# Multiplying the first tile's keys while the key and value weights are still being turned

## The chip, the cores and the metric

One NeuronCore of a Trainium2 chip runs the whole kernel as one launch. The metric is the device time of that launch in microseconds (us). All times of the profile are microseconds from the start of its span unless marked ns.

## The reference

One layer of a graph transformer over 3125 nodes of width 1024 and 50,000 edges. The part that matters here is the linear attention's key and value stage, which comes first in the kernel:

```
xn = layernorm(x)
K = elu(xn @ Wk.T + bk) + 1           # 16 heads of 64
V = xn @ Wv.T + bv
KV = einsum('phd,phe->hde', K, V);  Ksum = K.sum(over nodes)
# later: Q, the mix with Wo; a graph attention over the edges; a feed forward with
# a piecewise linear gelu; each added to x
```

The graph attention uses a dense 3125 x 3125 matrix of edge counts in DRAM. It is built beside the key and value stage: 39 MB are filled with zeros and then every edge is added by indirect DMAs.

## The kernel before

The kernel is a row of blocks. Within a block each engine runs its own program and engines meet only at semaphores; at the end of a block all engines meet, and none starts the next block before the last has drained. Three blocks matter.

**The preparation block** (line 494). The weights Wk and Wv come as 16 blocks of 128 rows x 1024 (8 of each), into a ring of five places in SBUF (`raw`). TensorE turns a block with 8 transposes into a place in PSUM (`SplitWeights.turn`, L428), ScalarE copies a rounded high part (`take_high`, L292), VectorE then takes the rest, the low part (`take_low`, L296). There are three PSUM places (`places=3`), so block r is turned only when the low part of block r-3 has been taken. SyncE loads blocks 5 to 15, each when the place in the ring is free (`load`). In the same block the first tile of 125 rows of x is normalised, turned (`turn_rows`, L283) and split (`take`, L476 and L292; the low part is L296 on `xT_space`), and the edges' keys are made and turned (L574). SyncE also broadcasts the biases bk and bv and loads the rows of tile 1 (L508 to L509).

**The key and value block** (line 589) runs over 25 tiles. For each, TensorE makes `k_ps` (`project`, 48 matmuls of 512 columns: 8 blocks x 3 products of high and low parts x 2 halves), half of `v_ps` (24), turns the next tile's rows (8 transposes), makes the other half of `v_ps` (24) and `kv` (8 pairs). VectorE normalises the next tile, adds biases, sums, and prepares one unit of edges a tile (`Edges.prepare`, its last instruction is L354). GpSimd first issues 50 zero fills of 764 KB each (L617, four in flight), then the diagonal (L621 and L624), and then 47 batches of edges, two batches to a unit, with four indirect DMAs each (`scatter_unit`, `scatter_batch`, L360 to L375). Batch n+1 waits until batch n has landed.

**The query block** (line 749) follows, with the rest of the edge batches.

PSUM in the preparation block: three places of two banks for blocks and `tr`, two banks. In the key and value block: `tr`, `k_ps`, `v_ps` and `kv`, two banks each.

Of the kernel before, what the change touches and what calls it, by code (L numbers as in the profile page):

```python
# [19 lines left out]
D = 1024  # L20
# [4 lines left out]
T = 125  # L25
NT = N // T
KB = D // 128
FB = F // 128
CH = 128
# [424 lines left out]
def keys_and_values(nc, st, a):  # L454
# [12 lines left out]
    stats, moments, root = sb("stats", [T, 2, 6]), sb("moments", [T, 2]), sb("root", [T, 5])  # L467
    x_loaded, xn_ready, stats_seen, first_link = [sem(f"x_loaded{i}") for i in range(2)], sem("xn_ready"), sem("stats_seen"), sem("first_link")
    turned, xT_copied, xT_high, xT_low, rows_loaded = sem("turned"), sem("xT_copied"), sem("xT_high"), sem("xT_low"), sem("rows_loaded")
    tr = ps("tr", [128, KB, 128])  # L470
    EARLY = 4

    def take(act, g, slot):

# [5 lines left out]
    with ExitStack() as pst:  # L480
        psb, pps, psem = allocators(nc, pst, "KP")
        spare_i = psb("spare_i", [CH, BATCH], I32)
        src_c, dst_c = (edges.row[0:CR, i * CB * CH:(i + 1) * CB * CH].bitcast(I32).rearrange("p (b c) -> p b c", b=CB) for i in range(2))
        key_c = edges.row[0:CR, 0:CB * CH].rearrange("p (b c) -> p b c", b=CB)
        zeros_set, ident_zeroed, ident_ready = psem("zeros_set"), psem("ident_zeroed"), psem("ident_ready")
        pads_set = psem("pads_set")
        masks_set, masks_ready, sums_zeroed = psem("masks_set"), psem("masks_ready"), psem("sums_zeroed")
        edges_loaded, keys_made, keys_turned, keys_copied = (
            psem("edges_loaded"), psem("keys_made"), psem("keys_turned"), psem("keys_copied"))
        keys_stored = a["keys_stored"]  # L490
        weights = SplitWeights(nc, pst, "KW", ((a["wk"], wk), (a["wv"], wv)), ident, [raw[:, i, :] for i in range(5)], places=3)
        blocks = range(2 * KB)

        with nc.Block() as block:  # L494
            @block.sync
            def _(sp):
                load_rows(sp, rows[:, 0, :], a["x"][0:T, :], x_loaded[0])
                for tile, e in ((src_c, a["src"]), (dst_c, a["dst"])):
                    most, whole = (CB - 1) * CR * CH, CHUNKS * CH
                    sp.dma_start(tile[:, 0:CB - 1, :], e[0:most].rearrange("(b c p) -> c b p", c=CR, p=CH)).then_inc(edges_loaded, 16)  # L500
                    sp.dma_start(tile[0:PADS, CB - 1, :], e[most:whole].rearrange("(c p) -> c p", p=CH)).then_inc(edges_loaded, 16)
                sp.wait_ge(pads_set, 2)
                for tile, e in ((src_c, a["src"]), (dst_c, a["dst"])):
                    sp.dma_start(tile[PADS:PADS + 1, CB - 1, 0:REST], e[whole:E].rearrange("(c p) -> c p", c=1)).then_inc(edges_loaded, 16)
                weights.load(sp, range(weights.ring, len(blocks)))
                for tile, row, n in ((bk_row, a["bk"], 12), (bv_row, a["bv"], 13)):
                    sp.wait_ge(weights.turned, n)
                    sp.dma_start(tile[:, :], row.partition_broadcast(T)).then_inc(rows_loaded, 16)  # L508
                load_rows(sp, rows[:, 1, :], rows_of(a["x"], 1), x_loaded[1])  # L509
                sp.wait_ge(keys_stored, 16)  # L510

            @block.gpsimd
            def _(pool):
                nc.gpsimd.memset(ident[:, :], 0.0).then_inc(ident_zeroed, 1)
                nc.gpsimd.memset(edges.mask[:, 0:BATCH - 1, :], AGAIN).then_inc(masks_set, 1)
                nc.gpsimd.memset(edges.mask[:, BATCH - 1:2 * BATCH - 1, :], 1.0).then_inc(masks_set, 1)
                nc.gpsimd.iota(spare_i[:, :], pattern=[[CH, BATCH]], base=N * N, channel_multiplier=1).then_inc(masks_set, 1)
                pool.wait_ge(ident_zeroed, 1)
                nc.gpsimd.affine_select(out=ident[:, :], in_=ident[:, :], compare_op=ALU.not_equal, fill=1.0,
                                        base=0, pattern=[[-1, 128]], channel_multiplier=1).then_inc(ident_ready, 1)  # L520
                pool.wait_ge(masks_set, 3)
                own = edges.mask[:, BATCH - 1, :]
                nc.gpsimd.affine_select(out=own, in_=own, compare_op=ALU.is_ge, fill=AGAIN,
                                        base=0, pattern=[[1, CH]], channel_multiplier=-1).then_inc(masks_ready, 1)
                nc.gpsimd.tensor_copy(edges.spare[:, :], spare_i[:, :]).then_inc(masks_ready, 1)
                nc.gpsimd.memset(kv_sum[:, :, :], 0.0).then_inc(sums_zeroed, 1)
                nc.gpsimd.memset(k_sum[:, :], 0.0).then_inc(sums_zeroed, 1)
                pool.wait_ge(keys_made, 1)
                pool.dma_start(a["keys_dram"].rearrange("(b c p) -> c b p", b=CB, p=CH), key_c[:, :, :]).then_inc(keys_stored, 16)
                pool.wait_ge(masks_ready, 2)  # L530
                pool.wait_ge(sums_zeroed, 2)

            @block.scalar
            def _(act):
                weights.load(act, range(weights.ring))
                weights.take_high(act, range(EARLY))
                take(act, 0, 0)
                weights.take_high(act, range(EARLY, KB))
                act.wait_ge(keys_turned, 1)
                nc.scalar.activation(edges.keys[:, :].rearrange("p (b c) -> p b c", b=CB), tr[0:CH, 0:CB, 0:CR], ACT.Copy).then_inc(keys_copied, 1)  # L540
                weights.take_high(act, range(KB, len(blocks)))
                act.wait_ge(zeros_set, 1)

            @block.vector
            def _(dve):
                nc.vector.memset(src_c[PADS:CR, CB - 1, :], N).then_inc(pads_set, 1)
                nc.vector.memset(dst_c[PADS:CR, CB - 1, :], 0).then_inc(pads_set, 1)
                nc.vector.memset(zeros[:, :], 0.0).then_inc(zeros_set, 1)
                chain = Chain(dve, first_link)
                dve.wait_ge(x_loaded[0], 32)  # L550
                normalise(nc, chain, rows[:, 0, :], rows[:, 0, :], stats, moments, root, stats_seen).then_inc(xn_ready, 1)
                weights.take_low(dve, range(EARLY // 2))
                dve.wait_ge(edges_loaded, 96)
                nc.vector.scalar_tensor_tensor(out=key_c[:, :, :], in0=src_c[:, :, :], scalar=float(N), in1=dst_c[:, :, :],
                                               op0=ALU.mult, op1=ALU.add).then_inc(keys_made, 1)
                weights.take_low(dve, range(EARLY // 2, EARLY))
                dve.wait_ge(xT_high, 1)
                low(nc, xT[:, 0, 1, :, :], xT_whole[:, :, :], xT[:, 0, 0, :, :]).then_inc(xT_low, 1)
                weights.take_low(dve, range(EARLY, len(blocks)))
                dve.wait_ge(keys_copied, 1)  # L560
                dve.wait_ge(xn_ready, 1)
                dve.wait_ge(weights.low_ready, len(blocks))

            @block.tensor
            def _(pe):
                pe.wait_ge(ident_ready, 1)
                weights.turn(pe, range(EARLY))
                pe.wait_ge(xn_ready, 1)
                turn_rows(nc, tr, rows[:, 0, :], ident, turned)
                weights.turn(pe, range(EARLY, KB))  # L570
                pe.wait_ge(xT_copied, 1)
                pe.wait_ge(keys_made, 1)
                for b in range(CB):
                    last = nc.tensor.transpose(tr[0:CH, b, 0:CR], key_c[:, b, :], ident[0:CR, 0:CR])  # L574
                last.then_inc(keys_turned, 1)
                weights.turn(pe, range(KB, len(blocks)))


    ones = sb("ones", [T, NT, 1])
    k_ps, v_ps, kv = ps("k_ps", [128, D]), ps("v_ps", [128, D]), ps("kv", [128, KB, 128])  # L580

    xT_stored = sem("xT_stored")
    k_done, v_done, kv_done = sem("k_done"), sem("v_done"), sem("kv_done")
    kb_ready, k_low, k_exp, k_ready, v_ready = sem("kb_ready"), sem("k_low"), sem("k_exp"), sem("k_ready"), sem("v_ready")
    ones_set, diagonal_set = sem("ones_set"), sem("diagonal_set")
    zero_filled = [sem(f"zero_filled{i}") for i in range(FILLS_AHEAD)]
# [2 lines left out]
    with nc.Block() as block:  # L589
# [99 lines left out]
        def _(pe):  # L689
            def body(g, n):  # L690
                xT_now = xT[:, n % 2, :, :, :]
                pe.wait_ge(xT_low, g + 1)
                project(nc, k_ps, xT_now, wk, k_done)
                project(nc, v_ps, xT_now, wv, v_done, (0,))
                if fixed(g, 0, NT - 2):
                    pe.wait_ge(xn_ready, g + 2)
# [6 lines left out]
                    cols = slice(pair * 128, (pair + 1) * 128)  # L703
                    m = nc.tensor.matmul(kv[:, pair, :], v[:, cols], k[:, cols], start=True, stop=True)
                m.then_inc(kv_done, 1)
            over_tiles(pe, body)


def linear_attention(nc, st, a):
# [1230 lines left out]
```

## Time and profile before

| | us |
|---|---|
| median of three runs | 3107.56 (3103.63 to 3111.19) |
| the profiled execution, its own time | 3111.14 |
| its span | 3109.0 |
| TensorE, busy share of the span | 98% |
| VectorE | 84% |
| ScalarE | 37% |
| GpSimd | 26% |

Busy shares are averages over the whole span. The change is in the first 50 us, and GpSimd is busy only in the first 1300 us, so the reading has to be by stage. An engine's queue (PEq, POOLq, SPq) has entries of its own: DRAIN is an engine that has reached the end of its block and waits for its own work to finish, EVENT_SEMAPHORE its release into the next block.

### The profile page before, as it was taken

To read this page: it belongs to the slowest core of one execution; us is meant where nothing else is said; L and a number is where in the kernel's file an instruction comes from. 1 tells how busy PE (TensorE), PEld (TensorE's weight loads), DVE (VectorE), ACT (ScalarE), POOL (GpSimd) and SP (SyncE) were. 2 spreads that over 40 slices of the span, in tenths; PEclk is the share of its full clock that TensorE was granted. 3 is DMA by queue.
4 is the path that set the end of the run, shared out by engine and by line. 5 is a ranking of instruction groups with operands and counts; after the bars stand their busy time and mean duration, and the time that the engine had idled before them with its cause. 6 is when DMAs were issued, how large, how long until landed. Compare 5 with 4: busy or idle time off the path is not lost. (4 is left out here: it accounts for less than half of the span.)

```text
span 3109.0 us, 41236 instructions
## 1 busy us (share of the span) xinstructions
PE 3037.5 (98%) x14012; PEld 2500.3 (80%) x14012; DVE 2604.5 (84%) x4513; ACT 1164.5 (37%) x1499; POOL 803.3 (26%) x716
## 2 busy tenths in 40 slices
PE   8999999989999999899999999999999999999998
PEld 6888888867888888677778888888888888878887
DVE  6777777767777777698989999999999988788886
ACT  3111111122111111233346566556656644565554
POOL 1256666754655666200000000000000000000000
PEclk9999999999999999999999999999999999999999
DMA  9943333353444444555655356447446634233331
GB/s 341 374 99 65 60 60 60 73 134 71 84 93 93 80 93 93 159 167 170 184 165 161 112 154 167 128 127 202 123 121 168 168 93 118 75 88 106 104 106 53
DMA packets 184432, 395.83 MB, mean 127 GB/s; under 512 B 78181, under 2 KB 79061, under 8 KB 184310
## 3 DMA queue, kind: packets, MB, share of 16 engines
q1 hardware_dynamic: 106230, 308.58, 33.6%
q0 software_dynamic: 71440, 65.24, 11.4%
q10 hardware_dynamic: 6640, 20.45, 2.0%
q8 instruction: 68, 1.11, 0.2%
q14 instruction: 54, 0.44, 0.0%
HBM read 303.36 MB, written 90.81 MB: 127 GB/s over the span
## 5 line engine op out<-in xcount | busy, mean ns | idle before, releaser
L1580 PE MATMUL G_acc<-values,whole_plain 125*125 125x257 f32 x5000 | 1095.9, 381 | 15.8 <-DVE whole_plain L1524 8.6
L1580 PEld LDWEIGHTS G_acc<-values,whole_plain 125*125 125x125 f32 x5000 | 935.4, 188 | 166.0 <-DVE whole_plain L1524 11.8
L375 POOL DMA_INDIRECT counts<-E_twins_now,E_cells_now x392 | 672.9, 1717 | 308.6 <-DMA counts<-E_twins_now,E_cells_now 171.3
L1424 ACT ACTIVATE whole_plain<-whole_plain,G_asrc_slope 125x750 f32<-125x750 f32 (+1 forms) x400 | 377.6, 945 | 388.3 <-DVE whole_plain L1511 387.3
L1511 DVE SCALAR_TENSOR_TENSOR whole_plain<-whole_plain,G_asrc_most 125x750 f32<-125x750 f32 (+1 forms) x400 | 409.5, 1024 | 32.8 <-PE G_acc L1580 31.7
L1396 POOL DMA_DIRECT2D gat<-xT_plain x100 | 53.7, 537 | 1027.4 <-ACT xT_plain L1440 1027.4
L268 PE MATMUL V_v_ps<-whole,xT_space 128*125 128x512 f32 x1200 | 285.1, 399 | 8.0 <-DVE xT_space L296 4.0
L268 PE MATMUL Q_mm<-Q_mixer,xT_space 128*125 128x512 f32 x1200 | 284.8, 396 | 5.5 <-DVE xT_space L296 5.5
L268 PE MATMUL K_k_ps<-whole,xT_space 128*125 128x512 f32 x1200 | 287.1, 398 | 3.2 <-PEq L494 3.2
L1052 DVE SCALAR_TENSOR_TENSOR N_least<-xT_plain,asrc_all,N_least 125x750 f32<-125x750 bf16 (+1 forms) x292 | 289.7, 992 | 0.0
L268 PE MATMUL K_v_ps<-K_wv,xT_space 128*125 128x512 f32 x1200 | 287.9, 395 | 0.0
L268 PE MATMUL Q_q_ps<-whole,xT_space 128*125 128x512 f32 x1200 | 287.4, 398 | 0.0
L1524 DVE SCALAR_TENSOR_TENSOR whole_plain<-whole_plain 125x750 f32<-125x750 f32 (+1 forms) x288 | 277.3, 963 | 6.8 <-ACT whole_plain L1424 4.5
L268 PEld LDWEIGHTS V_v_ps<-whole,xT_space 128*125 128x125 f32 x1200 | 221.5, 187 | 70.3 <-DVE xT_space L296 11.9
L268 PEld LDWEIGHTS Q_mm<-Q_mixer,xT_space 128*125 128x125 f32 x1200 | 223.6, 186 | 62.5 <-DVE xT_space L296 6.0
L343 DVE SCALAR_TENSOR_TENSOR E_scratch<-E_row,E_col,E_mask 128x512 bf16<-128x512 f32 x392 | 267.8, 747 | 1.7
L268 PEld LDWEIGHTS K_k_ps<-whole,xT_space 128*125 128x125 f32 x1200 | 221.7, 186 | 58.6 <-issue 3.4
L268 PEld LDWEIGHTS Q_q_ps<-whole,xT_space 128*125 128x125 f32 x1200 | 220.6, 185 | 56.7 <-issue 1.9
L268 PEld LDWEIGHTS K_v_ps<-K_wv,xT_space 128*125 128x125 f32 x1200 | 220.7, 186 | 53.3
L1740 ACT ACTIVATE whole<-F_work,F_knots 125x512 fp32r<-125x512 f32 x300 | 186.8, 709 | 47.3 <-PE F_bent_ps L1900 46.7
L634 ACT ACTIVATE K_raw<-K_raw 125x1024 f32<-125x1024 f32 x25 | 26.5, 1060 | 468.6 <-DVE K_raw L662 468.6
L1036 ACT ACTIVATE xT_plain<-whole_plain,N_huge 125x750 bf16<-125x750 f32 (+1 forms) x152 | 139.5, 918 | 32.4 <-DMA whole_plain<-counts 30.1
(195 smaller groups left out, 3178.2 us busy)
## 6 DMA issues: line engine op xcount, KB each, us to landing
whole_plain<-counts SPq DMA_DIRECT2D x279, 328.1 KB
counts<-wo_raw POOLq DMA_DIRECT2D x50, 763.5 KB, 9.7
whole_plain<-counts SPq DMA_DIRECT2D x68, 382.8 KB
xT_whole<-xnT SPq DMA_DIRECT2D x50, 500.0 KB, 3.7
E_row<-edge_keys ACTq DMA_DIRECT2D x26, 512.0 KB, 3.8
xnT<-xT_whole SPq DMA_DIRECT2D x25, 500.0 KB, 4.3
V_xT_other<-xnT SPq DMA_DIRECT2D x25, 500.0 KB, 4.0
gat<-xT_plain POOLq DMA_DIRECT2D x100, 125.0 KB, 2.5
```

Source lines behind the costliest of these rows:

```text
L268: last = nc.tensor.matmul(out, stationary(s, b), moving(m, b), start=(n == 0), stop=(n == len(terms) - 1))
L343: chain.step(nc.vector.scalar_tensor_tensor(out=self.scratch[:, c % 2, :], in0=batch, scalar=self.col[:, c:c + 1], in1=mask, op0=ALU.is_equal,
L375: nc.gpsimd.indirect_dma_start(out=counts_cells, out_offset=bass.IndirectOffsetOnAxis(ap=self.cells_now[:, slot, c:c + 1], axis=0), in_=se ...
L634: nc.scalar.activation(ex[:, :], ex[:, :], ACT.Exp).then_inc(k_exp, 1)
L1036: self.nc.scalar.activation(absent[:, n % 2, 0:w], counts[:, 0:w], ACT.Relu, bias=self.huge[:, :], scale=-ABSENT).then_inc(self.absent_rea ...
L1052: self.nc.vector.scalar_tensor_tensor(out=here, in0=mask, scalar=term, in1=here, op0=ALU.subtract, op1=ALU.min).then_inc(self.least_ready, 1)
L1396: pool.dma_start(a["gat_dram"][(at + t) * T:(at + t + 1) * T, h * C:(h + 1) * C], sums[:, t, 0:C]).then_inc(gat_stored, 16)
L1424: nc.scalar.activation(here, here, ACT.Exp, bias=asrc_slope[:, u % H, j:j + 1]).then_inc(exp_ready, 1)
L1511: nc.vector.scalar_tensor_tensor(out=weight[:, k % RING, 0:w], in0=rows[:, u % 2, 0, 0:w], scalar=asrc_most[:, u % H, j:j + 1], in1=rows[: ...
L1524: nc.vector.scalar_tensor_tensor(out=here, in0=here, scalar=1.0, in1=counts[:, 0:width(u)], op0=ALU.min, op1=ALU.mult).then_inc(weighted, 1)
L1580: m = nc.tensor.matmul(acc[0:T, t, 0:CW], weight[:, k % RING, t * T:(t + 1) * T], values[:, u % H, j, :], start=(j == 0), stop=(j == NT - 1))
L1740: nc.scalar.activation(terms[:, i, :], magnitude[:, n % 2, :], ACT.Relu, bias=knots[:, i:i + 1]).then_inc(terms_ready, 1)
```

## The change

The first tile's key product (48 matmuls) leaves the key and value block and is put between the turned blocks: ahead of each of the blocks 6 to 15 four products, and eight behind block 15. For this `k_ps` is allocated earlier, so the turned blocks have two PSUM places and no longer three. TensorE waits for the low part of the first tile before the first four products. The rows of tile 1 are loaded ahead of the last two weight blocks instead of behind the biases. The key and value block takes its first tile without the key product, and its loop for TensorE now leads with one tile and ends with two.

```diff
-    tr = ps("tr", [128, KB, 128])
-    EARLY = 4
+    tr, k_ps = ps("tr", [128, KB, 128]), ps("k_ps", [128, D])
+    k_done = sem("k_done")
+    EARLY, TAKEN = 4, 4
...
-        weights = SplitWeights(..., [raw[:, i, :] for i in range(5)], places=3)
+        weights = SplitWeights(..., [raw[:, i, :] for i in range(5)])          # places=2
+        def first_keys(pe, part):
+            for n in range(TAKEN * part, TAKEN * part + TAKEN):
+                half, i = n // (3 * KB), n % (3 * KB)
+                b, (s, m) = i // 3, ((0, 0), (0, 1), (1, 0))[i % 3]
+                if i == 0:
+                    pe.wait_ge(weights.low_ready, KB // 2 * (half + 1))
+                last = nc.tensor.matmul(k_ps[0:T, half * 512:(half + 1) * 512], xT[:, 0, s, b, 0:T], wk[:, half, m, b, :],
+                                        start=(i == 0), stop=(i == 3 * KB - 1))
+            if n == 6 * KB - 1:
+                last.then_inc(k_done, 1)
...
-                weights.load(sp, range(weights.ring, len(blocks)))
+                weights.load(sp, range(weights.ring, len(blocks) - 2))
+                load_rows(sp, rows[:, 1, :], rows_of(a["x"], 1), x_loaded[1])
+                weights.load(sp, range(len(blocks) - 2, len(blocks)))
...
-                load_rows(sp, rows[:, 1, :], rows_of(a["x"], 1), x_loaded[1])
...
-                weights.turn(pe, range(EARLY, KB))
-                pe.wait_ge(xT_copied, 1)
-                pe.wait_ge(keys_made, 1)
-                for b in range(CB):
-                    last = nc.tensor.transpose(tr[0:CH, b, 0:CR], key_c[:, b, :], ident[0:CR, 0:CR])
-                last.then_inc(keys_turned, 1)
-                weights.turn(pe, range(KB, len(blocks)))
+                weights.turn(pe, range(EARLY, EARLY + 2))
+                pe.wait_ge(xT_low, 1)
+                for r in range(EARLY + 2, len(blocks)):
+                    first_keys(pe, r - EARLY - 2)
+                    weights.turn(pe, range(r, r + 1))
+                    if r == KB - 1:
+                        ... the edges' keys turned, as above ...
+                for part in range(len(blocks) - EARLY - 2, 3 * KB // 2):
+                    first_keys(pe, part)
...
-                pe.wait_ge(xT_low, g + 1)
-                project(nc, k_ps, xT_now, wk, k_done)
+                if fixed(g, 1):
+                    pe.wait_ge(xT_low, g + 1)
+                    project(nc, k_ps, xT_now, wk, k_done)
...
-            over_tiles(pe, body)
+            over_tiles(pe, body, lead=1, tail=2)
```

## Rows read from the trace of the kernel before

**Rows 1.** Engines' queue entries at the end of the key and value block (L589).

```profile
L589 POOLq DRAIN  x1: 10580/10580/10580, 657.6 to 657.6; - x1
L589 DVEq DRAIN  x1: 17/17/17, 664.7 to 664.7; - x1
L589 PEldq EVENT_SEMAPHORE  x1: 51/51/51, 668.4 to 668.4; - x1
```

**Rows 2.** The timeline of GpSimd, start us, duration us, 36 to 174.

```profile
36.14 2.19 POOL L617 DMA_DIRECT2D counts<-wo_raw  x4 [20.03 <-issue]
...
158.87 0.53 POOL L617 DMA_DIRECT2D counts<-wo_raw  x1 [2.39 <-DMA counts<-wo_raw]
159.40 1.43 POOL L621 DMA_DIRECT2D counts<-K_ones  x1
170.77 0.69 POOL L624 DMA_DIRECT2D counts<-K_ones  x1 [9.95 <-DMA counts<-wo_raw]
173.14 0.18 POOL L360 COPY E_cells_now<-E_cells 128x8 uint32<-128x8 uint32 x1 [1.67 <-DMA counts<-K_ones]
```

**Rows 3.** The same timeline: copies that open a unit, among them the last.

```profile
465.04 1.19 POOL L360 COPY E_cells_now<-E_cells 128x8 uint32 x1
...
488.00 0.79 POOL L360 COPY E_cells_now<-E_cells 128x8 uint32 x1
...
508.41 0.91 POOL L360 COPY E_cells_now<-E_cells 128x8 uint32 x1
...
653.36 0.77 POOL L360 COPY E_cells_now<-E_cells 128x8 uint32<-128x8 uint32 x1
```

**Rows 4.** The timeline of VectorE: the last unit that this block's batches need.

```profile
643.70 0.17 DVE L354 TENSOR_TENSOR E_cells<-E_moved,E_col 128x8 uint32<-128x8 f32 x1
```

**Rows 5.** The timeline of TensorE in the preparation block and after it.

```profile
6.51 5.23 PE L428 MATMUL KW_tr<-ident,K_raw 128*128 128x128 f32 x24 [6.51 <-DMA K_raw<-in_L_mix_Wk]
12.90 1.07 PE L428 MATMUL KW_tr<-ident,K_raw 128*128 128x128 f32 x8 [1.16 <-issue]
13.80 1.02 PE L283 MATMUL K_tr<-ident,K_rows 125*128 125x125 f32 x8
...
30.43 1.09 PE L428 MATMUL KW_tr<-ident,K_raw 128*128 128x128 f32 x8 [0.99 <-DMA K_raw<-in_L_mix_Wv]
34.73 12.98 PE L268 MATMUL K_k_ps<-whole,xT_space 128*125 128x512 f32 x48 [3.20 <-PEq L494]
47.54 2.69 PE L268 MATMUL K_v_ps<-K_wv,xT_space 128*125 128x512 f32 x11
```

**Rows 6.** The timeline of VectorE in the preparation block.

```profile
11.58 2.35 DVE L296 TENSOR_TENSOR whole<-KW_tr,whole 128x1024 fp32r<-128x1024 f32 x2
...
17.04 1.19 DVE L296 TENSOR_TENSOR xT_space<-xT_whole,xT_space 128x1000 fp32r<-128x1000 f32 x1
...
32.62 1.22 DVE L296 TENSOR_TENSOR K_wv<-KW_tr,K_wv 128x1024 fp32r<-128x1024 f32 x1 [0.86 <-ACT K_wv L292]
```

**Rows 7.** The timeline of ScalarE in the preparation block.

```profile
14.92 1.01 ACT L476 ACTIVATE xT_whole<-K_tr 128x1000 f32<-128x1000 f32 x1
```

**Rows 8.** TensorE's timeline in a tile of the key and value block.

```profile
538.29 11.41 PE L268 MATMUL K_k_ps<-whole,xT_space 128*125 128x512 f32 x48
549.54 5.71 PE L268 MATMUL K_v_ps<-K_wv,xT_space 128*125 128x512 f32 x24
555.10 1.02 PE L283 MATMUL K_tr<-ident,K_rows 125*128 125x125 f32 x8
555.87 5.77 PE L268 MATMUL K_v_ps<-K_wv,xT_space 128*125 128x512 f32 x24
```

**Rows 9.** Queue entries at the end of the preparation block (L494).

```profile
L494 PEldq EVENT_SEMAPHORE  x1: 51/51/51, 34.4 to 34.4; - x1
```

**Rows 10.** Windows: length; busy time and count per engine; clock; DMA share; GB/s.

```profile
16.00:18.00 2.00, 1.84 (x15) 1.66 (x16) 2.00 (x2) 2.00 (x3) 0.10 (x1) 1.00 1.02 379
36.00:38.00 2.00, 2.00 (x6) 1.54 (x5) 0.00 (x0) 0.00 (x0) 1.86 (x4) 0.50 0.65 238
30.40:34.40 4.00, 1.09 (x8) 0.85 (x8) 2.55 (x3) 1.12 (x2) 0.00 (x0) 1.00 0.38 120
36.14:44.40 8.26, 8.26 (x32) 6.54 (x31) 0.00 (x0) 0.00 (x0) 2.19 (x4) 0.84 0.93 335
44.40:158.87 114.47, 114.47 (x547) 93.28 (x546) 83.40 (x202) 15.55 (x15) 24.82 (x46) 1.00 1.01 376
```

More of the change, by code:

```diff
@@ L490, in keys_and_values @@
         keys_stored = a["keys_stored"]
-        weights = SplitWeights(nc, pst, "KW", ((a["wk"], wk), (a["wv"], wv)), ident, [raw[:, i, :] for i in range(5)], places=3)
+        weights = SplitWeights(nc, pst, "KW", ((a["wk"], wk), (a["wv"], wv)), ident, [raw[:, i, :] for i in range(5)])
         blocks = range(2 * KB)
+        def first_keys(pe, part):
[8 more added lines that the diff above has]
+                last.then_inc(k_done, 1)
         with nc.Block() as block:
@@ L569, in _ @@
                 turn_rows(nc, tr, rows[:, 0, :], ident, turned)
-                weights.turn(pe, range(EARLY, KB))
-                pe.wait_ge(xT_copied, 1)
-                pe.wait_ge(keys_made, 1)
-                for b in range(CB):
-                    last = nc.tensor.transpose(tr[0:CH, b, 0:CR], key_c[:, b, :], ident[0:CR, 0:CR])
-                last.then_inc(keys_turned, 1)
-                weights.turn(pe, range(KB, len(blocks)))
+                weights.turn(pe, range(EARLY, EARLY + 2))
[4 more added lines that the diff above has]
+                    if r == KB - 1:
+                        pe.wait_ge(keys_made, 1)
+                        for b in range(CB):
+                            last = nc.tensor.transpose(tr[0:CH, b, 0:CR], key_c[:, b, :], ident[0:CR, 0:CR])
+                        last.then_inc(keys_turned, 1)
+                for part in range(len(blocks) - EARLY - 2, 3 * KB // 2):
+                    first_keys(pe, part)
     ones = sb("ones", [T, NT, 1])
-    k_ps, v_ps, kv = ps("k_ps", [128, D]), ps("v_ps", [128, D]), ps("kv", [128, KB, 128])
+    v_ps, kv = ps("v_ps", [128, D]), ps("kv", [128, KB, 128])
     xT_stored = sem("xT_stored")
-    k_done, v_done, kv_done = sem("k_done"), sem("v_done"), sem("kv_done")
+    v_done, kv_done = sem("v_done"), sem("kv_done")
     kb_ready, k_low, k_exp, k_ready, v_ready = sem("kb_ready"), sem("k_low"), sem("k_exp"), sem("k_ready"), sem("v_ready")
```

## The prediction

> **What bounds the kernel now.** The page says TensorE is busy 98% of the span, and the change takes TensorE work out of a stage in which TensorE is full. That invites the answer "so many microseconds of TensorE saved". I read the stages instead, asking at each block's end which engine came last. The queue entries at the end of the key and value block give it [rows 1]: VectorE reaches its drain at 664.7, but GpSimd's drain lasts from 657.6 to 657.6 + 10.6 = 668.2, and TensorE is let into the next block at 668.4. So this block ends with GpSimd, 3.5 us after everybody else. Then I followed GpSimd back. It waits for nothing that VectorE makes: its last unit is copied at 653.36 [rows 3], 9.7 us after VectorE finished that unit at 643.70 [rows 4]. Units follow each other by their own landing times, from 173.14 on [rows 2]. Before that come the zero fills, from 36.14 on, and the DMA engines are full while they run (share 1.01, 376 GB/s) [rows 10]. And the first fill is held by one thing only, the end of the preparation block at 34.4 [rows 9]. So up to 668 the chain that sets the time is: preparation block, 50 fills, 47 batches of edges, drain. TensorE has 3.5 us to spare on it. After 668.4 all engines restart together and nothing of the change is left, so the total moves by what 668.2 moves.
>
> The question is therefore not how much TensorE saves but **when the preparation block ends**.
>
> **The preparation block, part by part.** Durations first. Eight transposes cost 0.9 us when they follow others (12.90 to 13.80 [rows 5]); a product of 512 columns costs (549.54 - 538.29) / 48 = 0.234 us, and between halves of `v_ps` the transposes fit in 555.87 - 555.10 = 0.77 us, so changing between the two kinds costs nothing visible [rows 8]. High and low part together end 2.3 us after a block's last transpose: 30.43 + 1.09 = 31.52 to 32.62 + 1.22 = 33.84 [rows 5, 6]; the release follows 0.56 us later, at 34.4 [rows 9].
>
> *Two places instead of three.* Block 2 now waits for the low part of block 0, about 12.8 (half of the pair that starts at 11.58 [rows 6]), so it is turned 12.9 to 13.8; block 3 waits for the low part of block 1 at 11.58 + 2.35 = 13.93, and is turned 14.0 to 14.9; the first tile's rows follow, 14.9 to 15.8. In the profile these rows were turned from 13.80 on, and ScalarE took them at 14.92 [rows 5, 7]. Now ScalarE has block 3 first, to about 16.0, then the two copies of 1.0 us each, and VectorE's 1.2 us end near 19.3, where the profile has 17.04 + 1.19 = 18.23 [rows 6]. First products at 19.4.
>
> *Products between the blocks.* From 19.4 TensorE has 48 x 0.234 = 11.25, ten blocks x 0.9 = 9.0 and the edges' keys, 0.35 (half of eight transposes' 0.77, a little less): 20.6 us. Blocks landed and were turned by 31.5 before; now block 15 is turned when all but the last eight products (1.9 us) are done: 19.4 + 20.6 - 1.9 = 38.1. High and low part, 2.3: 40.4. Release, 0.56: 41.0, so 6.6 us later than 34.4. I add 1 us for places where two blocks' products (2 x 0.94) and one block (0.9) leave the high and low parts, 2.3 plus a semaphore each way, almost no room. **The block ends near 42.0, 7.6 us later.** Below: if the products cost nothing, the two places alone hold each second block for 0.9 + 2.3 + 0.15 = 3.35 us; block 6 cannot be turned before 20.5, block 14 not before 20.5 + 4 x 3.35 = 33.9, block 15 ends near 36.5 and the release is near 39.4: +5. Above: before 12 us the transposes ran at 5.23 / 24 = 0.218 us each and at 12.90 at half of that [rows 5]; with only two blocks turned in a row at first and then a pause, blocks 2 and 3 and the rows may still run slow, up to +2.5 on the first products: +10.
>
> The Trainium skill ("TensorE: Matmul & The Clock Gate", Back-to-back issue gap) states a sustained 131 ns for a matmul of 512 columns paired with its weight load. The trace shows 234 ns here [rows 8]. By the page's figure the products would cost 6.3 us, TensorE would no longer bound the interleaving, and the block would end by the two places' bound above, near +5 to +6.
>
> *What is hidden.* The weights' loads are issued as places come free; before they bound the block, now each has at least 1.8 us, and 0.52 MB at 376 GB/s takes 1.4, so they are off the chain. The rows of tile 1 are queued ahead of blocks 14 and 15, 1.4 us of transfer that is covered for the same reason (TensorE reaches those blocks after 35). On SyncE's queue the biases wait for blocks 11 and 12 to be turned, now about 31 and 33 instead of 25 and 26; they move slowly (120 GB/s with only them and the rows under way [rows 10]), 1.0 MB in 8.5 us, and land by about 42; VectorE waits for them before the first tile, which costs nothing, as TensorE's first value half runs 5.6 us.
>
> *What TensorE saves.* Values of tile 0 start at 42.0 + 0.3 = 42.3 and not at 47.54 [rows 5]: 5.2 us. In 12.98 us for 48 products the profile also held a slow start, at a granted clock of 0.50 in 36 to 38 [rows 10], which the change removes. All of this ends in front of the same drain: TensorE and VectorE arrive some 5 us earlier and wait for GpSimd some 12 us longer.
>
> **GpSimd.** Its first fill moves from 36.14 to 43.7. The fills are bound by the DMA engines. For them: the leftovers of biases and rows no longer share the first microseconds, where the rate was 335 instead of 376 GB/s [rows 10]: 8.26 x 41 / 376 = 0.9 us. Against them: tile 1 and all later tiles run about 13 us sooner against the fills, and a tile moves 1.5 MB in 25 us, so 0.8 MB more share the stretch, 2.1 us at 376 GB/s. I take nothing, and keep -1 to +2. The scatters are a chain of landings; most units take 20.4 us, but one in five or six takes about 23 (465.04 to 488.00, against 20.41 for the next [rows 3]), when its batches meet a tile's transfers. With another phase one such meeting more or fewer is possible: -3 to +3.
>
> **Sum.** Against the profiled execution: 3111.14 + 7.6 = 3118.7, against the median, 3.6 lower: 3107.56 + 7.6 = **3115.2 us**.
>
> **The rivals.**
> *TensorE's saving counts* (the other side). If GpSimd made good its late start, the block would end with VectorE, at 664.7 - 5.2 = 659.5 instead of 668.2: 8.7 faster, 3098.9. The mechanism would be fills that run faster once nothing of the preparation is in their way. It decides from 7.6 us regained on: 5.6% of the 134.6 us from 36.14 to 170.77 [rows 2]. Against it stands the share of 1.01 for 114 of these; 0.9 us can be seen. Chance 0.05.
> *Partly absorbed*: block end near +5, one slow unit fewer, the fills' 0.9: +1 to +6.2. The time would be about 3111.5. For it: each term has such an end. Chance 0.29.
> *The clock stays low between transposes.* If transposes did not keep the clock up, the interleaving would run at half rate: products at the pace of 36 to 38, 6 in 2 us or 0.33 each [rows 10], and transposes at 0.218: 48 x 0.10 + 80 x 0.11 = 13.6 more, 3129. The granted clock was 1.00 while the engine did nothing but transposes [rows 10], and they reached 0.11 us by themselves [rows 5]. Chance 0.04. The Trainium skill says that transposes do not raise the clock (same page, Part 4: PE-mode transpose); this trace shows otherwise.
> *My forecast*, +6.2 to +13: 0.62.
>
> **How the numbers follow.** About 0.2%, 6.2 us, is what a measurement of this kernel can tell from no change. Slower by more: 0.62 + 0.04 = 0.66. Within: 0.29. Faster: 0.05. The likeliest case by itself reaches from +5 - 1 to +10 + 3, 3111.5 to 3120.5. For 8 in 10 the range takes in most of the absorbed case below and the upper ends together above: 3108 to 3122.
>
> **What would show it.** Right: the end of the preparation block near 42, the first fill 1.7 us behind it, TensorE's first value product near 42.3, scatters from about 181, GpSimd's drain ending near 676 with the others waiting since about 659, and every later block as long as before. Wrong: a preparation block that ends before 39.5 or after 45; fills much shorter than 134.6 us; VectorE's drain last at the end of the key and value block.

## The result and the profile after

The changed kernel took 3117.59 us (median of 15 runs, 3109.79 to 3121.85) beside 3107.7 for the kernel before (15 runs): ratio 1.003, 95% interval 1.0023 to 1.0038. It is slower, and the forecast was 3115.2. Measured again later the same kernel came out nearer: 1.0000, 1.0005 and 1.0008, none of them clear of no change (below). What follows keeps both facts.

The profiled execution took 3115.1 us, span 3112.9. The two block ends, in the engines' queue entries (duration in ns, start in us), as in [rows 9] and [rows 1]:

```profile
L507 PEldq EVENT_SEMAPHORE  x1: 51/51/51, 43.7 to 43.7; - x1
```

```profile
L608 POOLq DRAIN  x1: 10605/10605/10605, 662.5 to 662.5; - x1
L608 DVEq DRAIN  x1: 17/17/17, 664.0 to 664.0; - x1
L608 PEldq EVENT_SEMAPHORE  x1: 51/51/51, 673.2 to 673.2; - x1
```

The preparation block is released 9.3 us later. The key and value block ends with GpSimd's drain at 662.5 + 10.6 = 673.1, 4.9 us later, and 9 us after VectorE. Behind it nothing changed: 3112.9 - 673.2 = 2439.7 us, and 3109.0 - 668.4 = 2440.6 before. So the difference of the two profiled executions, 3.9 us of span, sits in front of that drain. It is not the 9.9 us between the medians: the profiled 3111.14 lies near the top of the 15 runs of the kernel before (3100.57 to 3111.58), and 3115.1 is the fourth fastest of the 15 of the changed kernel. GpSimd's timeline, for [rows 2]:

```profile
45.47 2.19 POOL L636 DMA_DIRECT2D counts<-wo_raw  x4 [29.49 <-issue]
...
166.15 0.53 POOL L636 DMA_DIRECT2D counts<-wo_raw  x1 [2.77 <-DMA counts<-wo_raw]
166.68 1.43 POOL L640 DMA_DIRECT2D counts<-K_ones  x1
176.86 0.70 POOL L643 DMA_DIRECT2D counts<-K_ones  x1 [8.76 <-DMA counts<-wo_raw]
179.13 0.18 POOL L360 COPY E_cells_now<-E_cells 128x8 uint32<-128x8 uint32 x1 [1.57 <-DMA counts<-K_ones]
```

First fill +9.3 us, first unit only +6.0: the fills took 133.7 us instead of 137.0. From the first unit to the drain's end it is 494.0 instead of 495.1. TensorE's timeline, for [rows 5]:

```profile
6.90 3.65 PE L428 MATMUL KW_tr<-ident,K_raw 128*128 128x128 f32 x16 [6.90 <-DMA K_raw<-in_L_mix_Wk]
13.04 3.65 PE L428 MATMUL KW_tr<-ident,K_raw 128*128 128x128 f32 x16 [2.50 <-issue]
16.48 1.87 PE L283 MATMUL K_tr<-ident,K_rows 125*128 125x125 f32 x8
18.15 2.04 PE L428 MATMUL KW_tr<-ident,K_raw 128*128 128x128 f32 x16
21.76 1.19 PE L502 MATMUL K_k_ps<-whole,xT_space 128*125 128x512 f32 x4 [1.56 <-DVE xT_space L296]
22.94 1.06 PE L428 MATMUL KW_tr<-ident,K_raw 128*128 128x128 f32 x8
...
39.82 1.03 PE L428 MATMUL KW_tr<-ident,K_raw 128*128 128x128 f32 x8
40.61 2.11 PE L502 MATMUL K_k_ps<-whole,xT_space 128*125 128x512 f32 x8
43.81 5.80 PE L268 MATMUL K_v_ps<-K_wv,xT_space 128*125 128x512 f32 x24 [1.09 <-PEq L507]
50.34 1.07 PE L283 MATMUL K_tr<-ident,K_rows 125*128 125x125 f32 x8 [0.73 <-DVE K_rows L204]
...
59.76 0.49 PE L724 MATMUL K_kv<-K_raw 125*128 125x128 f32 x2 [1.91 <-DVE K_raw L690]
```

Read it in four steps. The pause of 2.5 us ahead of 13.04 is the two places. The 16 transposes behind it take 3.65 us, 0.22 each, twice those from 18.15 on. From 21.76 the interleaving runs almost without a gap (block 14, at 37.95, starts 0.2 us later than the pace of the others) until block 15 is turned at 39.82 + 1.03 = 40.85. And in the first tile TensorE waits for VectorE twice, 0.73 and 1.91 us, where the kernel before had no wait. VectorE's own timeline names the cause of the first wait, the broadcast of the second bias:

```profile
45.37 1.29 DVE L176 BATCH_NORM_STATS2 K_stats<-K_rows 125x6 f32<-125x512 f32 x2 [1.43 <-DMA K_raw<-in_L_mix_bv]
```

### The profile page after: what moved, and what is told of

Same layout as the page of the kernel before. It is cut to its first block and busy times, and to the rows that moved or that the text cites. A ratio compares the mean times of both kernels' runs of the same rounds, so it can differ in the third digit from the quotient of the medians.

```text
span 3112.9 us, 41230 instructions
## 1 busy us (share of the span) xinstructions
PE 3038.8 (98%) x14012; PEld 2503.5 (80%) x14012; DVE 2606.5 (84%) x4513; ACT 1166.4 (37%) x1499; POOL 803.3 (26%) x716
## 3 DMA queue, kind: packets, MB, share of 16 engines
q0 software_dynamic: 71440, 65.24, 11.1%
## 5 line engine op out<-in xcount | busy, mean ns | idle before, releaser
L268 PE MATMUL K_k_ps<-whole,xT_space 128*125 128x512 f32 x1152 | 274.1, 396 | 0.0
L268 PEld LDWEIGHTS K_k_ps<-whole,xT_space 128*125 128x125 f32 x1152 | 211.8, 185 | 52.5
```

What stands on the lines that cost most here:

```text
L268: last = nc.tensor.matmul(out, stationary(s, b), moving(m, b), start=(n == 0), stop=(n == len(terms) - 1))
```

## The experiments

Each was timed beside the kernel before on the same chip; the kernels of one group below shared a chip, and each group had another. The table gives what the one trace of each shows, in us from the span's start; a drain's end is its start plus its duration. "After" is the changed kernel.

| trace | first product | release | first fill | first unit | GpSimd's drain ends | VectorE's drain | span |
|---|---|---|---|---|---|---|---|
| before | 34.73 | 34.4 | 36.14 | 173.1 | 668.2 | 664.7 | 3109.0 |
| after | 21.76 | 43.7 | 45.47 | 179.1 | 673.1 | 664.0 | 3112.9 |
| again | 19.38 | 41.1 | 42.84 | 175.4 | 663.7 | 662.5 | 3102.3 |
| again, 2 | 21.95 | 44.0 | 45.77 | 176.7 | 667.7 | 668.2 | 3106.6 |
| again, 3 | 21.07 | 42.7 | 44.49 | 178.1 | 671.1 | 662.3 | 3110.4 |
| after, 46 batches | 21.05 | 42.7 | 44.49 | 176.8 | 656.0 | 664.5 | 3102.0 |
| before, 46 batches | 35.05 | 34.7 | 36.46 | 171.5 | 652.3 | 664.8 | 3108.0 |
| before, two places | 42.08 | 41.7 | 43.49 | 174.0 | 669.8 | 672.0 | 3111.6 |
| after, 46, pause filled | 19.96 | 41.7 | 43.50 | 175.7 | 654.9 | 662.6 | 3102.3 |
| after, fills ahead | 21.11 | 51.5 | 33.36 | 177.6 | 664.5 | 671.4 | 3108.0 |
| after, 46, rows late | 22.02 | 43.7 | 45.46 | 178.8 | 657.5 | 666.1 | 3105.6 |
| together (45) | 19.71 | 41.4 | 43.17 | 174.0 | 645.1 | 661.1 | 3100.7 |
| before, 48 batches | 34.33 | 34.0 | 35.74 | 171.7 | 683.5 | 665.1 | 3123.2 |
| after, 48 batches | 21.04 | 42.7 | 44.49 | 176.3 | 677.0 | 664.0 | 3118.6 |

Two spreads of this table are the measure for what follows. What is left of the span behind the end of the key and value block is 2436.5 to 2443.1 us. And VectorE's drain comes 619.6 to 624.2 us after the release in the seven traces of the changed kernel whose edits leave the first tile alone (47, 46 and 48 batches, and the pause filled).

**First group, one chip.**

*The changed kernel again*, no edit.

> The changed kernel once more, nothing edited, to see how much of its distance from the kernel before belongs to the stage up to the end of the key and value block. Theory (GpSimd's chain sets the time until the key and value block ends): the preparation block is released near 43.7, GpSimd's drain ends near 673 and 4 to 10 us after that of the kernel before, VectorE's is done near 664; the ratio is 1.003. The medians of the first measurement lay 9.9 us apart and the two profiled executions only 4.0; this run is to tell whether another trace shows the missing 6 us before 673 (the fills and edges chain varies from run to run) or after it (a slower clock or longer stages later). Rival (the time is lost by TensorE, elsewhere): the distance sits in stages after the key and value block.

Median 3105.87 (3102.04 to 3117.94), ratio 1.000 (0.999 to 1.001). The expected 1.003 did not come back, and the drain did not end near 673:

```profile
L608 POOLq DRAIN  x1: 10670/10670/10670, 653.0 to 653.0; - x1
L608 DVEq DRAIN  x1: 17/17/17, 662.5 to 662.5; - x1
L608 PEldq EVENT_SEMAPHORE  x1: 51/51/51, 663.9 to 663.9; - x1
```

The same kernel ended this block 9.3 us earlier than in its other trace, and the rest of the span is 3102.3 - 663.9 = 2438.4, within 1.3 us of the other. Where its time differs between these two traces is GpSimd's chain: 2.6 us from a release at 41.1, 1.1 from the fills, 5.8 from the scatters (488.2 against 494.0). The 2.6 come from the start:

```profile
12.87 2.20 PE L428 MATMUL KW_tr<-ident,K_raw 128*128 128x128 f32 x16 [2.34 <-issue]
14.90 1.02 PE L283 MATMUL K_tr<-ident,K_rows 125*128 125x125 f32 x8
16.35 2.20 PE L428 MATMUL KW_tr<-ident,K_raw 128*128 128x128 f32 x16 [0.43 <-issue]
19.38 1.19 PE L502 MATMUL K_k_ps<-whole,xT_space 128*125 128x512 f32 x4 [0.83 <-DVE xT_space L296]
```

Here the transposes after the pause are fast, and the first product is at 19.38, where the working of the prediction had put it (19.4).

*46 batches instead of 47*, in the changed kernel and in the kernel before.

```diff
-BATCHES_K = 47
+BATCHES_K = 46
```

> The changed kernel with BATCHES_K = 46 instead of 47: one batch of edges, about 10 us of GpSimd's work, moves out of the key and value block into the query block, where GpSimd has waited for VectorE. Theory: GpSimd's drain then ends at 673 - 10 = 663, VectorE's at 664 is the last, the block ends near 664.3, and the kernel is 8 to 9 us faster than the changed one, 0 to 4 us faster than the kernel before (TensorE's saving of some 4 us at last counts). Rival (GpSimd's drain was only the last by appearance, TensorE or the query block bounds): within 2 us of the changed kernel.

Median 3105.94 (3102.78 to 3108.95), ratio 0.9995 (0.9986 to 1.0003).

> The kernel before with BATCHES_K = 46. Theory: its key and value block ends with VectorE at 664.7 instead of GpSimd's drain at 668.2, so 3.5 us faster than the kernel before, and what is between this run and the changed kernel with 46 is what TensorE's part of the change is worth by itself, some 4 us by where the values of the first tile start (43.8 against 47.5). Rival: no change.

Median 3107.62 (3103.80 to 3112.79), ratio 0.9999 (0.999 to 1.0008). In both traces the block now ends with VectorE, with GpSimd done 8.5 and 12.5 us before it:

```profile
L608 POOLq DRAIN  x1: 10706/10706/10706, 645.3 to 645.3; - x1
L608 DVEq DRAIN  x1: 17/17/17, 664.5 to 664.5; - x1
```

```profile
L589 POOLq DRAIN  x1: 10677/10677/10677, 641.6 to 641.6; - x1
L589 DVEq DRAIN  x1: 17/17/17, 664.8 to 664.8; - x1
```

What follows from this is less than it seems. The traces show that 46 batches take GpSimd off the end of the block. The times do not show a gain: the changed kernel with 46 batches (3105.94) equals the changed kernel with 47 on the same chip (3105.87), where 8 to 9 us had been expected against the first measurement. Its runs lie closer together (3103 to 3109, against 3102 to 3118), but the 46 batches of the second group spread from 3101 to 3115, so the scatter of the runs is not shown to be that chain's.

The kernel before gained only about 1 us from 46, where 3.5 was expected. In its trace the block did end 3.5 us earlier (664.9 against 668.4), and the rest of the span was 2.5 us longer (2443.1 against 2440.6). Adding back half a unit's 20.4 us, its chain would have ended at 652.3 + 10.2 = 662.5, 2.3 us ahead of VectorE; the trace with 48 batches below, less the same 10.2, gives 673.3. These are estimates, and they put the 668.2 of [rows 1] in the middle of a race that either side can win. And VectorE's drain is at 664.5 and 664.8: TensorE's saving is gone before the end, even with nothing hidden.

*Two places and nothing else*, in the kernel before.

```diff
-        weights = SplitWeights(..., [raw[:, i, :] for i in range(5)], places=3)
+        weights = SplitWeights(..., [raw[:, i, :] for i in range(5)])
```

> The kernel before with two PSUM places for turned blocks instead of three, and nothing else: the first tile's key product stays in the key and value block. Theory: the two places alone hold each second block for about 3.35 us (turn 0.9, high and low part 2.3, semaphores), so the preparation block ends near 40.5 instead of 34.4 although TensorE has hardly anything to do in it, GpSimd's chain moves by 6 and the kernel is about 6 us slower; most of the delay is then the price of the places and not of the products. Rival (the products between the blocks cost the time, the third place is hardly used): the block ends within 1 us of 34.4 and the time is the same.

Median 3113.57 (3108.84 to 3116.71), ratio 1.0015 (1.0006 to 1.0023). The release is at 41.7, +7.3 without one product between the blocks. TensorE's timeline shows the hold, a period of 3.48 us for two blocks (3.35 expected):

```profile
26.22 2.19 PE L428 MATMUL KW_tr<-ident,K_raw 128*128 128x128 f32 x16 [0.95 <-issue]
29.71 2.19 PE L428 MATMUL KW_tr<-ident,K_raw 128*128 128x128 f32 x16 [1.29 <-DVE K_wv L296]
33.19 2.20 PE L428 MATMUL KW_tr<-ident,K_raw 128*128 128x128 f32 x16 [1.29 <-DVE K_wv L296]
```

In the changed kernel's traces the release comes 6.7 to 9.6 us later, so most of that is the price of the third place; the products only fill the gaps it leaves. The path expected for the time was wrong here: GpSimd's drain moved by 1.6 us (669.8), not by 6, and the block ended with VectorE at 672.0, 7.3 us later, because in this kernel the key product starts later too. On the same chip it is 7.7 us slower than the changed kernel, which pays for the places as well but has the key product out of the way.

**Second group, another chip.**

*The changed kernel a third time.*

> The changed kernel a third time, since two measurements of it gave ratios of 1.003 and 1.000. Theory: the distance to the kernel before is a race of two chains at the end of the key and value block. TensorE's and VectorE's chain ends at 662.5 to 664 whatever happens; GpSimd's ended at 663.7 and 673.1 in the two traces. So the ratio lies between 0.999 and 1.003, this trace's GpSimd drain ends between 663 and 674, and the span minus that block's end is 2438 to 2442. Rival (two chips, or two states of one, differ in the later stages): the later stages are longer by several us in the slower case.

Median 3108.51 (3102.98 to 3114.87), ratio 1.0005 (0.9996 to 1.0014). GpSimd's drain was inside the expected range, but both chains ended level, 667.7 and 668.2: that VectorE's would end at 662.5 to 664 "whatever happens" is a miss of 4 us. TensorE's longest wait in that block, and what followed it:

```profile
PE K_tr L283 <- DVE K_rows L204: 3.8, 1, 3.8
```

```profile
53.72 1.93 PE L283 MATMUL K_tr<-ident,K_rows 125*128 125x125 f32 x8 [3.84 <-DVE K_rows L204]
55.30 7.92 PE L268 MATMUL K_v_ps<-K_wv,xT_space 128*125 128x512 f32 x24
```

The same transposes and products take 1.07 and 5.77 us in the changed kernel's first trace. The granted clock is 0.50 from 53.7 to 56.0 here and back at 1.00 from 60.0. So the wait was paid twice, 3.8 us standing and then about 2.9 us at the lower clock.

*The pause filled*, with 46 batches.

```diff
-                weights.turn(pe, range(EARLY))
+                weights.turn(pe, range(2))
+                for _ in range(24):
+                    nc.tensor.transpose(tr[:, 0, :], ident[:, :], ident[:, :])
+                weights.turn(pe, range(2, EARLY))
```

> The changed kernel with 46 batches and 24 added transposes of the identity between blocks 1 and 2, where TensorE otherwise pauses for 2.5 us (their result is overwritten unread). It asks whether the slow transposes of blocks 2 and 3 (0.22 us each in the profile of the changed kernel, 0.11 in its second trace) come from that pause. Theory: with the pause filled they run at 0.11 us always, the first products start at 19.4 instead of up to 21.8, the preparation block is released at 41.1 or before, and with GpSimd's chain out of the way the kernel is 0 to 2.6 us faster than the same with 46 batches, 1.5 in the middle. Rival (the speed of the first transposes has another cause): the first products start anywhere from 19.4 to 21.8 as before, and the added transposes cost nothing or delay block 2 by up to a few us.

```profile
10.41 3.44 PE L583 MATMUL K_tr<-ident 128*128 128x128 f32 x24
13.69 1.91 PE L428 MATMUL KW_tr<-ident,K_raw 128*128 128x128 f32 x16
15.44 1.02 PE L283 MATMUL K_tr<-ident,K_rows 125*128 125x125 f32 x8
...
19.96 1.20 PE L502 MATMUL K_k_ps<-whole,xT_space 128*125 128x512 f32 x4 [0.61 <-DVE xT_space L296]
```

Blocks 2 and 3 now take 1.91 us instead of 3.65, and again 1.91 in the other kernel with the filling (*Together*, below). With the pause of 2.3 to 2.7 us they took 2.95 to 3.65 us in eight of nine traces and 2.20 in one. In the three traces with three places, where the pause is 1.1 to 1.9 us, block 3 took 1.07 us and less. So the pause is the cause, though not in every execution. The 24 ran until 13.7 and held block 2 back by 0.7 us: first product at 19.96, release at 41.7, neither as early as expected. The time, 3106.51, ratio 1.0000 (0.9991 to 1.0009), cannot tell it from the same without.

*Fills issued inside the preparation block*, 47 batches.

```diff
+                pool.wait_ge(zeros_set, 1)
+                pool.wait_ge(weights.turned, 12)
+                for n in range(FILLS_AHEAD):
+                    pool.dma_start(a["counts_fill"][n, :, :], zeros[:, :]).then_inc(zero_filled[n], 16)
...
-            for n in range(ZN):
+            for n in range(FILLS_AHEAD, ZN):
```

> The changed kernel, 47 batches, but GpSimd issues its first four zero fills in the preparation block as soon as block 11 has been turned (near 33), not after that block's end. Theory (the chain begins with the fills and they wait for nothing but the block's end): 3.1 MB of the 39 MB are written while the DMA engines are at a third of their rate, the first unit is copied some 8 us earlier (168 to 171 instead of 175 to 179), GpSimd's drain ends before 664 and VectorE's is last near 663, so it is 0 to 9 us faster than the changed kernel, on a par with 46 batches. Rival: no change against the changed kernel, or slower because the last weight blocks and the biases are delayed by the fills.

Median 3112.18 (3106.96 to 3117.08), ratio 1.0013 (1.0004 to 1.0022): a miss. The fills were issued from 33.36 on, but the block did not end before they had landed:

```profile
L508 POOLq DRAIN  x1: 16685/16685/16685, 34.6 to 34.6; - x1
L508 DVEq DRAIN  x1: 10/10/10, 43.3 to 43.3; - x1
L508 PEldq EVENT_SEMAPHORE  x1: 51/51/51, 51.5 to 51.5; - x1
```

GpSimd's drain lasted 16.7 us, to 51.3, and the other engines stood 8 us for it. The last of the four fills was issued at 35.0 and landed 16.0 us later, at 51.0, so here GpSimd's drain at a block's end lasts as long as the transfers that it has issued. They were slow at their end only: of their 3.1 MB, 2.8 had moved by 44.0 (share 1.02 from 36 to 40), and the rest crept along beside the biases at a share of 0.30 to 0.34. The first unit was copied at 177.6 and GpSimd's drain ended at 664.5, inside what the changed kernel does anyway. What made this kernel slower is the other chain: released 8 us late, VectorE reached its drain at 671.4 and ended the block.

*The rows of tile 1 loaded behind the biases again*, 46 batches.

```diff
-                weights.load(sp, range(weights.ring, len(blocks) - 2))
-                load_rows(sp, rows[:, 1, :], rows_of(a["x"], 1), x_loaded[1])
-                weights.load(sp, range(len(blocks) - 2, len(blocks)))
+                weights.load(sp, range(weights.ring, len(blocks)))
...
+                load_rows(sp, rows[:, 1, :], rows_of(a["x"], 1), x_loaded[1])
```

> The changed kernel with 46 batches and the rows of tile 1 loaded where the kernel before loads them, behind the biases. Theory: the biases are broadcast slowly (0.12 MB per us) and the rows queue behind them, so they land some 4 to 8 us later than needed; TensorE waits for the normalised rows after the first value half, 0.7 us in the changed kernel, about 5 here, TensorE's chain is not hidden behind GpSimd's with 46 batches, and the block ends some 4 us later than with the rows sooner. Rival (the order of the loads makes no difference): the same time within 1 us.

```profile
48.06 1.29 DVE L176 BATCH_NORM_STATS2 K_stats<-K_rows 125x6 f32<-125x512 f32 x2 [4.13 <-DMA K_rows<-in_x]
```

```profile
53.03 1.93 PE L283 MATMUL K_tr<-ident,K_rows 125*128 125x125 f32 x8 [3.46 <-DVE K_rows L204]
```

Statistics start at 48.06 instead of 45.37, TensorE waits 3.46 us instead of 0.73, and VectorE's drain comes 622.4 us after the release instead of 620.3 (the changed kernel's trace, same release). But the same kernel with the rows sooner shows waits of 0.7 to 3.8 us and 619.6 to 624.2, so neither figure stands out of its spread, and the expected 4 us are not there. Median 3108.69, ratio 1.0004 (0.9995 to 1.0013): not told apart by time either.

**Third group.** *Together*: 45 batches, the pause filled, and VectorE's wait for the biases placed ahead of their first use.

```diff
-            dve.wait_ge(rows_loaded, 32)
             ahead_of_tiles(chain)
...
+                if not fixed(g, 1):
+                    dve.wait_ge(rows_loaded, 32)
                 dve.wait_ge(k_done, g + 1)
```

> The changed kernel with 45 batches, the 24 filling transposes, and VectorE's wait for the biases moved from ahead of the first tile to ahead of the first use of a bias. In all traces of the changed kernel TensorE waited 0.7 to 3.8 us for the normalised rows of tile 1 after its first value half, and VectorE began to normalise them only when the second bias had landed (near 45.4), 1.5 to 4.4 us after the block's start. Theory (that wait is what eats TensorE's saving inside the key and value block): the normalisation starts right after the release, TensorE's wait goes to under 0.5 us, VectorE's drain comes 617 to 619 us after the release instead of 620 to 624, near 659.5, with GpSimd's drain before it, and the kernel is 2 to 4 us faster than the same with 46 batches and the filling transposes, 3 to 6 us faster than the kernel before. Rival (the rows themselves land that late, or another wait takes its place): VectorE's drain stays 620 to 622 us after the release.

```profile
41.52 5.78 PE L268 MATMUL K_v_ps<-K_wv,xT_space 128*125 128x512 f32 x24 [1.10 <-PEq L507]
47.14 1.02 PE L283 MATMUL K_tr<-ident,K_rows 125*128 125x125 f32 x8
...
57.16 1.16 PE L728 MATMUL K_kv<-K_raw 125*128 125x128 f32 x8 [2.58 <-DVE K_raw L694]
```

The wait for the rows is gone, and a wait of 2.58 us for the second half of the values takes its place. VectorE's drain is at 661.1, 619.7 after the release, 1.2 us better than with the pause filled alone (662.6, 620.9), but the changed kernel's fourth trace has 619.6 with none of these edits. Median 3107.81 (3100.15 to 3112.12), ratio 0.9997 (0.9988 to 1.0006): no gain over the kernel before that this measurement can show.

*The changed kernel a fourth time*, on the same chip.

> The changed kernel a fourth time, beside the one above. Theory (two chains race at the end of the key and value block, VectorE's near 662 to 668, GpSimd's near 664 to 673): a ratio between 0.999 and 1.003, and the end of that block in the trace between 663 and 674. Rival (the first measurement's 1.003 is the value): 1.003.

Median 3110.94 (3103.35 to 3117.50), ratio 1.0008 (0.9997 to 1.0019); the block ended at 671.2, with GpSimd, VectorE's drain at 662.3.

**Fourth group.** *48 batches* (the edit as above, with 48), to have both kernels bound by GpSimd beyond doubt.

> The kernel before with one batch of edges more in the key and value block (48). It makes GpSimd's chain the longer one without doubt, where with 47 it ended level with VectorE's or up to some us behind it. Theory (the longer chain ends the block): GpSimd's drain ends at 672 to 678, VectorE's at 664.7, and the kernel is 8 to 11 us slower than the kernel before, a ratio of 1.0025 to 1.0035. Rival (GpSimd is not what ends the block): no change.

Median 3120.32 of 9 runs (3113.09 to 3136.14), ratio 1.0044 (1.0028 to 1.006). GpSimd's drain ended at 672.7 + 10.8 = 683.5, VectorE's stood at 665.1.

> The changed kernel with 48 batches. Between this and the kernel before with 48, both bound by GpSimd's chain, stands what the change does to that chain alone: the release and the first fill 6.6 to 9.3 us later, fills 3 us shorter (132 against 136 in the traces so far), the same batches. Theory: GpSimd's drain ends 3 to 6 us after that of the kernel before with 48, and the medians lie 3 to 6 us apart. Rival (the first measurement, 9.9 us, is the change's price when GpSimd binds): 9 to 10 us apart. Rival two (TensorE's saving counts): no slower than the other with 48.

Median 3128.49 of 6 runs (3120.81 to 3131.39), ratio 1.0067 (1.0054 to 1.0081). One batch more costs the kernel before 13 us, more than the 8 to 11 expected, so its block does end with GpSimd's chain when that is the longer. Between the two kernels with 48 the medians are 8.2 us apart and the means 5.6 (3127.1 and 3121.5), with nine and six runs that spread over 23 and 11 us and ratios whose intervals overlap: this does not decide between 3 to 6 and 9 to 10. The two traces go the other way:

```profile
L589 POOLq DRAIN  x1: 10777/10777/10777, 672.7 to 672.7; - x1
L608 POOLq DRAIN  x1: 10724/10724/10724, 666.3 to 666.3; - x1
```

The changed kernel's drain ends at 677.0, 6.5 us ahead of the 683.5 of the kernel before, where 3 to 6 us behind was expected. Its release is 8.7 us later, its fills are 4.1 shorter, and its chain from the first unit to the drain is 11.1 shorter for the same batches (500.7 against 511.8). That chain varies by more than the change moves, so one trace of each cannot size the change.

## Why the prediction was right, and where it was off

**The bound.** That GpSimd's chain can end the key and value block is shown: it came last in three of the changed kernel's four traces with 47 batches and in both with 48, and the 48th batch cost the kernel before 13 us. That it stood 3.5 us behind everybody in the kernel before was one trace. Over the traces its chain from first unit to drain took 488.2 to 494.0 us in the changed kernel, 495.1 in the kernel before (495.8 with two places); I had allowed 3 us either way. Before, the two chains are near a tie; after, GpSimd's came last in three of four traces, by 1.2, 8.8 and 9.1 us. VectorE's came last in the third trace, which the prediction had named as a sign of being wrong. So the mechanism holds for the kernel that was profiled, and the size is a range: the kernel is slower by what GpSimd's chain happens to lose to VectorE's.

**The sum.** Forecast +7.6 at the block's end, all of it from the release. In the profiled execution it is +9.3 from the release, -3.3 from the fills and -1.1 from the scatters, +4.9, and -0.9 behind it; the medians moved by +9.9. That 3117.6 came so near the forecast 3115.2 is in part luck. The same kernel measured 3105.9, 3108.5 and 3110.9 later, the first of them below the range that was given, and the profiled executions lie 4.0 us apart where 7.6 was forecast.

**The release.** Forecast 42.0; the changed kernel's traces give 43.7, 41.1, 44.0 and 42.7. First product to last turned block is 40.85 - 21.76 = 19.1 us, forecast 18.7, so of the 1 us that I added for tightness 0.4 was needed; half of that is block 14, whose load stood behind the rows of tile 1 and which I had called covered (TensorE waits 0.15 us for that block's transfer in the third trace). The slow transposes after the pause, put only into the upper bound, were there in three of four traces, for up to 2.6 us. The interleaving kept the pace of [rows 8]: four products and eight transposes take 29.52 - 27.72 = 1.80 us, 1.84 by the forecast. The 131 ns that the Trainium skill states for a matmul of 512 columns ("TensorE: Matmul & The Clock Gate", Back-to-back issue gap) had no part in it. The Trainium skill ("TensorE: Matmul & The Clock Gate", Part 4: PE-mode transpose) says that transposes do not raise the clock. That is at odds with the rows of the filled pause: 40 transposes in a row behind 16 at 0.23 us, the last 16 at 0.12. The profile lists them as MATMUL; whether they run in the mode that the page means, no row shows.

**The fills.** Taken as unchanged, with -1 to +2; they became shorter, 133.7, 132.6, 130.9 and 133.6 against 137.0, and 135.0 and 136.0 in the other traces that keep three places (46 and 48 batches). The term was mis-sized by some 3 us. It does not come from the moved products: the kernel before with two places, which has none, took 130.5. The DMA rate over the stretch from the fifth fill to the last shows it:

```profile
55.50:166.15 110.65, 108.74 (x525) 88.76 (x524) 82.00 (x203) 13.65 (x14) 23.97 (x46) 1.00 1.01 385
```

385 GB/s against 376 in [rows 10] at the same share of 1.01; 382 and 383 in the other two traces with three places, 388 in the kernel before with two. So 376 is the low end of the kernels before. Why the same share moves more was not tried, nor whether the later start or the two places bring it.

**TensorE's saving.** This step failed, though the time did not hang on it. I said TensorE and VectorE would arrive some 5 us earlier (values of tile 0 at 42.3 instead of 47.54). The values did start 3.7 us earlier (43.81), but VectorE's drain came only 0.7 earlier, 664.0 against 664.7. In the first tile TensorE has 24 products instead of 72 ahead of the turned rows, so nothing hides VectorE's normalisation any more (in the kernel before VectorE began it 10 us after the release, at 44.41, and TensorE turned the rows at 53.09 without a wait): I had costed the biases' late landing at nothing because "the first value half runs 5.6 us", and forgot that behind the biases stand 4.9 us of normalising. It cost TensorE 0.7 to 3.8 us, and a second wait, for the values' sum ahead of `kv`, up to 1.9; in the third trace also 2.9 us at the lower clock behind the wait. Because GpSimd was last in the profiled execution, this error did not show in its time.

**The biases** move slowly because few engines carry them: with only them under way, from 40 to 44 us in the changed kernel's first trace, the DMA share is 0.30 to 0.34. The Trainium skill ("DMA: Bandwidth & Descriptors", Why a DMA increments its semaphore by 16 and not by 1) says that a copy runs on as many engines as the largest number up to 16 that divides the outer dimension of both its sides. Worked out from that rule, 125 rows give 5 of 16, or 0.31. The trace agrees; a split of the broadcast was not tried.

**What stays open.** The first measurement lies 9.9 us above the kernel before, three later ones -2.9, +1.3 and +3.2 us. The one trace of the first is 4.8 us later at the block's end and explains half; it is also one of the faster of its 15 runs. If the others had GpSimd's drain still later, it would fit, but there is no trace of them. Later stages that differ by several us, the rival named for the third measurement, are not in the four traces: 2438.2 to 2439.7 us behind the block's end. The later measurements were on three different chips, so what a chip adds is not separated.

## What to carry to other kernels

Ask of each block which engine came last, in the engines' drains, before crediting any engine with a saving; and ask it of several executions, since a chain that is last by 3 us in one trace may tie in the next. Work pulled ahead of a block's release is paid by every chain that starts at that release, here 39 MB of fills on an engine that has nothing to do with the work. A buffer given up for the pulled work has its own price: two places instead of three moved the release by 7.3 us before a single product was added. Work taken out of a tile also takes away the cover of what ran beside it.

## What the runs showed of the hardware

A drain at the end of a block waits for transfers that GpSimd has issued: 16.7 us with four fills under way, and with that a block in which every other engine had been done for 8 us.

Transposes after a pause of 2.5 us ran at 0.22 us each for all or part of the next 24, against 0.11 to 0.12 otherwise, in three of the changed kernel's four traces. The granted clock shows it in only one of the three, the fourth measurement:

```profile
15.00:20.00 5.00, 4.60 (x30) 4.17 (x28) 2.64 (x4) 3.45 (x5) 0.94 (x1) 0.76 0.93 307
```

In half-microsecond windows it stands at 0.50 from 14.5 to 17.0 there; in the other two it stands at 1.00, and only the instruction times tell. A wait in the middle of a block can cost the same way: behind the 3.84 us of the third trace the granted clock was 0.50, and 24 products took 7.92 us instead of 5.77. It does not always happen: behind 3.54 us in the second trace they took 5.77.
